# Two node blocks at a time in the node stage of a graph layer

## What is computed

```python
h = maximum(layernorm(x), 0)
edge_in_f = concat([h[src], h[dst], edge_attr]);  msgs_f = relu(edge_in_f @ W1_f + b1_f) @ W2_f + b2_f
agg = segment_sum(msgs_f, dst)
edge_in_r = concat([h[dst], h[src], edge_attr]);  msgs_r = relu(edge_in_r @ W1_r + b1_r) @ W2_r + b2_r
agg = agg + segment_sum(msgs_r, src)
x = x + (h + relu(concat([agg, h]) @ Wn1 + bn1) @ Wn2 + bn2)
```

## Time and profile before

| | us |
|---|---|
| median of three runs | 1609.94 (1607.84 to 1611.34) |
| the profiled execution | 1610.51 |
| its span | 1608.8 |
| PE, PEld busy | 1280.4, 970.6 |
| DVE, ACT, POOL busy | 972.0, 942.1, 1103.2 |

### The profile page before, as it was taken

How to read it: one execution, slowest core, us unless ns; L and a number is a source line. 1 busy time by engine, 2 the same in 40 slices (tenths; PEclk the granted TensorE clock), 3 DMA queues, 4 the chain that set the end, 5 groups by cost and what they waited for, 6 DMA issues and landing times.

```text
span 1608.8 us, 29477 instructions
## 1 busy us (share of the span) xinstructions
PE 1280.4 (80%) x7070; PEld 970.6 (60%) x7070; DVE 972.0 (60%) x3294; ACT 942.1 (59%) x2256; POOL 1103.2 (69%) x1003
## 2 busy tenths in 40 slices
PE   5899998457877778887787877778888756899998
PEld 4677777335655555665565656556666544666665
DVE  7999999426666666666666666666666641222222
ACT  4888888345555555555545555555555524677776
POOL 7888888888888888888888888888888761000000
PEclk9999999768788887778778788887777887999999
DMA  6899998425555555555555555555555547999998
GB/s 214 288 312 315 312 316 290 141 51 111 109 111 111 111 105 104 104 105 105 104 104 105 105 102 100 103 103 103 104 102 101 101 71 235 345 353 343 347 342 298
DMA packets 238410, 281.00 MB, mean 175 GB/s; under 512 B 53170, under 2 KB 155200, under 8 KB 238348
## 3 DMA queue, kind: packets, MB, share of 16 engines
q1 hardware_dynamic: 168408, 241.57, 45.2%
q0 software_dynamic: 68992, 38.59, 20.5%
q10 hardware_dynamic: 948, 0.30, 0.1%
HBM read 162.62 MB, written 117.72 MB: 174 GB/s over the span
## 4 chain that ended last, share of the span: by engine, by line
POOL 33%; issue 22%; DMA 15%; PE 4%; DVE 3%; ACT 1%; POOLq 0%; SPq 0%; DVEq 0%; ACTq 0%
POOL table L532 28%; DMA out_x<-ncentred 12%; POOL got_odd L514 6%; DMA table<-to_send,scatter_at 2%; DVE ncentred L1138 2%; DVE same L979 1%; PE bank L833 1%; PE bank L871 1%; DMA same<-table 1%; PE bank L820 1%; PE bank L882 0%; PE bank L818 0%; SPq L392 0%; PE bank L804 0%; PE bank L892 0%
## 5 line engine op out<-in xcount | busy, mean ns | idle before, releaser
L532 POOL DMA_INDIRECT table<-to_send,scatter_at x392 | 622.6, 1588 | 134.0 <-issue 118.4
L846 PEld LDWEIGHTS bank<-message,same 128*128 128x128 f32 x1960 | 270.3, 222 | 44.2 <-issue 39.2
L846 PE MATMUL bank<-message,same 128*128 128x128 f32 x1960 | 290.9, 313 | 4.8 <-DVE message L1011 4.8
L639 ACT ACTIVATE nh<-nx,all_sums,all_rstd 128x64 f32<-128x64 f32 x784 | 280.2, 434 | 0.1
L514 POOL DMA_INDIRECT got_even<-in_x,gather_first x196 | 212.9, 1086 | 39.8 <-issue 34.7
L775 PE MATMUL bank<-wn_h,nturned 128*128 128x256 f32 x784 | 196.7, 394 | 31.7 <-ACT nhidden L683 24.1
L514 POOL DMA_INDIRECT got_odd<-in_x,gather_at x180 | 180.2, 1001 | 54.9 <-issue 54.0
L804 PE MATMUL bank<-ident,h_ends 128*128 128x128 f32 x196 | 52.0, 359 | 198.7 <-DVE h_ends L1020 192.6
L979 DVE TENSOR_SCALAR_CACHE_REDUCE same<-others,ids 128x128 f32<-128x128 int32 (+3 forms) x392 | 190.7, 543 | 12.7 <-issue 7.9
L818 PE MATMUL bank<-turned,w_ends 128*128 128x256 f32 x392 | 167.1, 516 | 37.9 <-ACT turned_edge L609 37.9
L775 PEld LDWEIGHTS bank<-wn_h,nturned 128*128 128x128 f32 x784 | 143.1, 192 | 67.9 <-issue 36.2
(11 more groups left out here) (79 smaller groups left out, 1984.3 us busy)
## 6 DMA issues: line engine op xcount, KB each, us to landing
nx<-in_x SPq DMA_DIRECT2D x194, 256.0 KB
table<-nhidden SPq DMA_DIRECT2D x97, 512.0 KB
same<-table SPq DMA_DIRECT2D x97, 512.0 KB, 5.4
others<-numbers SPq DMA_DIRECT2D x196, 128.0 KB
out_x<-ncentred SPq DMA_DIRECT2D x97, 256.0 KB, 4.4
nx<-out_x SPq DMA_DIRECT2D x55, 256.0 KB, 4.8
out_x<-nh SPq DMA_DIRECT2D x31, 256.0 KB
table<-to_send,scatter_at POOLq DMA_INDIRECT x392
```

Of the source, the lines that this page charges most:

```text
L532: pool.indirect_dma_start(table, bass.IndirectOffsetOnAxis(ap=scatter_at[s][:, k:k + 1], axis=0), to_send[s][:, k, :], None, compute_op=AL ...
L639: last = act.activation(nh[s][:, g, :], nx[place][:, g, :], ACT.Relu, bias=all_sums[:, at, g:g + 1].rearrange("p a g -> p (a g)"), scale=a ...
L846: last = pe.matmul(bank[6 + s][:, k * M:(k + 1) * M], same[s][:, o, k * P:(k + 1) * P], message[s][:, o, :], start=(o == k), stop=(o == KB ...
```

## The change

Blocks are handled in pairs. Partition p of a pair of blocks holds 16 consecutive nodes: the first 8 belong to block 2i, the others to block 2i + 1. In the node stage SP loads a pair of blocks with one transfer of 512 KB (4 KB for each partition) and stores the table rows of a pair with one of 1 MB (8 KB for each partition). The loads go to four pair buffers `x_pair` in the space of `same`, the rows to four pair buffers `rows_pair` in the space of `kept_more`; `zeros` moves behind them. The first pair is loaded as two single blocks, so that block 0 has its own semaphore. SP loads a pair eight blocks ahead and stores a pair two blocks behind. The last pair has 1696 nodes on LASTP = 106 partitions. The other two stages still move single blocks, now as the halves of a pair. The loops of SP, ACT and DVE in the node stage are unrolled by eight. The diff, cut to its core:

```diff
-    LASTP = (N - (NW - 1) * WIN) // G
+    LASTP = (N - (NW - 2) * WIN) // (2 * G)
+    XRING = 8
...
-        zeros = kept_more[:, 0:2, :].rearrange("p a c -> p (a c)")[:, 0:ZC]
+        rows_pair = [kept_more[:, 4 * p:4 * p + 4, :].rearrange("p a c -> p (a c)") for p in range(XRING // 2)]
+        x_pair = ntab
+        zeros = kept_more[:, 16:18, :].rearrange("p a c -> p (a c)")[:, 0:ZC]
...
-                Step(NW, 0).do(load_x_begin, 0, ring=NRING)
+                for s in range(2):
+                    load_window(x, 0, s, x_pair[0][:, s * G * D:(s + 1) * G * D], b_x_first if s == 0 else b_x[0])
                 load_ends(sp, SRC, src)
...
-                for k in range(1, 6):
-                    Step(NW, 0).do(load_x_begin, k, ring=NRING)
+                for k in range(2, XRING, 2):
+                    Step(NW, 0).do(load_x_begin, k, ring=XRING)
...
-            def last_rows(a):
-                return a[(NW - 1) * WIN:N, :].rearrange("(p g) d -> p (g d)", g=G)
+            def pair_rows(a, i):
+                rows = a[(NW - 2) * WIN:N, :] if is_last(i) else a[bass.ds(i * (2 * WIN), 2 * WIN), :]
+                return rows.rearrange("(p h g) d -> p h (g d)", h=2, g=G)
+
+            def parts(i):
+                return LASTP if is_last(i) else P
 
             def load_window(a, i, s, to, landed):
-                if is_last(i, s):
-                    sp.dma_start(to[0:LASTP, :], last_rows(a)).then_inc(landed, 16)
-                else:
-                    sp.dma_start(to, node_rows(a, i, s)).then_inc(landed, 16)
+                sp.dma_start(to[0:parts(i), :], pair_rows(a, i)[:, s, :]).then_inc(landed, 16)
 
             def store_window(a, i, s, of, stored):
...
+                sp.dma_start(pair_rows(a, i)[:, s, :], of[0:parts(i), :]).then_inc(stored, 16)
...
             def load_x_begin(i, s, turn, place):
                 if not first(turn):
-                    sp.wait_ge(b_centred[s], i - 1)
-                load_window(x, i, s, flat(nx[place]), b_x[place])
+                    for q in range(2):
+                        sp.wait_ge(b_centred[q], i - XRING // 2 + 1)
+                sp.dma_start(x_pair[place // 2][0:parts(i), :], pair_rows(x, i).rearrange("p h c -> p (h c)")
+                             ).then_inc(b_x[place // 2], 16)
...
-            def store_rows(i, s):
-                sp.wait_ge(b_rows[s], 2 * (i + 1))
-                store_window(table[0:N, :], i, s, nhidden[s][:, :], b_stored[s])
+            def store_rows(i, s, turn, place):
+                for q in range(2):
+                    sp.wait_ge(b_rows[q], 2 * (i + 1))
+                sp.dma_start(pair_rows(table[0:N, :], i).rearrange("p h c -> p (h c)"),
+                             rows_pair[place // 2][0:parts(i), :]).then_inc(b_stored[place // 2], 16)
 
             def begin(w):
-                w.do(load_x_begin, 6, ring=NRING)
+                if w.n % 2 == 0:
+                    w.do(load_x_begin, XRING, ring=XRING)
...
-                w.do(store_rows, -1)
+                if w.n % 2 == 0:
+                    w.do(store_rows, -2, ring=XRING)
...
-            run(sp, NW, [(4, 88, 4)], 1, begin)
+            run(sp, NW, [(XRING, 88, XRING)], 1, begin)
...
-                    for q in range(2):
-                        pool.wait_ge(b_stored[q], 16 * (NW // 2))
+                    for q in range(XRING // 2):
+                        pool.wait_ge(b_stored[q], 16 * len(range(q, NW // 2, XRING // 2)))
...
-                    if not first(i):
-                        act.wait_ge(b_stored[s], 16 * i)
-                    act.copy(nhidden[s][:, half * 512:(half + 1) * 512], bank[2 + 2 * s + half][:, :]
-                             ).then_inc(b_rows[s], 1)
+                    if not first(turn):
+                        act.wait_ge(b_stored[place // 2], 16 * turn)
+                    c = (2 * s + half) * 512
+                    act.copy(rows_pair[place // 2][:, c:c + 512], bank[2 + 2 * s + half][:, :]).then_inc(b_rows[s], 1)
```

More of the change, by code:

```diff
@@ L111, in gnn_layer @@
     MORE_FROM = KEPT - MORE
-    assert NW % 2 == 0 and N % G == 0 and G * D == 2 * KB * D and 2 * KEPT <= PAIRS and 4 * KEPT <= NB
+    assert NW % 2 == 0 and N % (2 * G) == 0 and G * D == 2 * KB * D and 2 * KEPT <= PAIRS and 4 * KEPT <= NB
     table = nc.dram_tensor("table", (ROWS, M), F32, kind="Internal").ap()
@@ L255, in gnn_layer @@
         s_loads_held = sem("loads_held")
-        b_x = [sem(f"b_x_in{p}") for p in range(NRING)]
+        b_x = [sem(f"b_x_pair_in{p}") for p in range(XRING // 2)]
+        b_x_first = sem("b_first_x_in")
         b_sums = sems("b_sums_ready")
@@ L269, in gnn_layer @@
         b_rows = sems("b_rows_ready")
-        b_stored = sems("b_rows_stored")
+        b_stored = [sem(f"b_rows_pair_stored{p}") for p in range(XRING // 2)]
         e_means = sem("e_scaled_means_ready")
@@ L371, in load, with is_last @@
                                  ).then_inc(s_others[s], 16)
[L373 to L377, removed]
-            def last_rows(a):
-                return a[(NW - 1) * WIN:N, :].rearrange("(p g) d -> p (g d)", g=G)
+            def is_last(i):
+                return isinstance(i, int) and i == NW // 2 - 1
+            def pair_rows(a, i):
[3 more added lines that the diff above has]
+                return LASTP if is_last(i) else P
             def load_window(a, i, s, to, landed):
-                if is_last(i, s):
-                    sp.dma_start(to[0:LASTP, :], last_rows(a)).then_inc(landed, 16)
-                else:
-                    sp.dma_start(to, node_rows(a, i, s)).then_inc(landed, 16)
+                sp.dma_start(to[0:parts(i), :], pair_rows(a, i)[:, s, :]).then_inc(landed, 16)
             def store_window(a, i, s, of, stored):
[L389 to L392, removed]
+                sp.dma_start(pair_rows(a, i)[:, s, :], of[0:parts(i), :]).then_inc(stored, 16)
             def flat(a):
@@ L692, in begin @@
                     square(0, 0)
-                w.do(copy_rows(0), -1)
-                w.do(copy_rows(1), -1)
+                w.do(copy_rows(0), -1, ring=XRING)
+                w.do(copy_rows(1), -1, ring=XRING)
             for k in range(3):
@@ L702, in _ @@
                     copy_begin(0, 0)
-            run(act, NW, [(4, 92, 4)], 1, begin)
+            run(act, NW, [(XRING, 88, XRING)], 1, begin)
             run(act, NB, [(4, 96, 4)], 2, batch)
@@ L1053, in of_window, with x_window @@
                 return a[:, bass.ds(2 * i + s, 1), :].rearrange("p a g -> p (a g)")
+            def x_window(place):
+                half = place % 2
+                return x_pair[place // 2][:, half * G * D:(half + 1) * G * D].rearrange("p (g d) -> p g d", d=D)
             def sum_begin(i, s, turn, place):
-                dve.wait_ge(b_x[place], 16 * (turn + 1))
-                dve.tensor_reduce(of_window(all_sums, i, s), nx[place][:, :, :], AX.X, ALU.add).then_inc(b_sums[s], 1)
+                if first(turn) and place == 0:
+                    dve.wait_ge(b_x_first, 16)
+                else:
+                    dve.wait_ge(b_x[place // 2], 16 * (turn + 1))
+                dve.tensor_reduce(of_window(all_sums, i, s), x_window(place), AX.X, ALU.add).then_inc(b_sums[s], 1)
             def centre_begin(i, s, turn, place):
@@ L1097, in _ @@
             for k in range(3):
-                Step(NW, 0).do(sum_begin, k, ring=NRING)
-                Step(NW, 0).do(centre_begin, k, ring=NRING)
+                Step(NW, 0).do(sum_begin, k, ring=XRING)
+                Step(NW, 0).do(centre_begin, k, ring=XRING)
                 if k == 0:
@@ L1108, in _ @@
             dve.memset(zeros, 0.0).then_inc(s_zeros, 1)
-            run(dve, NW, [(4, 92, 4)], 0, begin)
+            run(dve, NW, [(XRING, 88, XRING)], 0, begin)
             centre(Step(NB, 0), 0)
```

10 lines of the change are left out of this document (4 added, 6 removed).

## The result

The changed kernel takes 1645.85 us (median; 1644.73 to 1646.32) where the kernel before took 1608.89 on the same chip: a ratio of 1.0227 with a 95% interval of 1.0209 to 1.0244, slower by 37.0 us. Forecast were 1638.0 and slower, with a range to 1648: sign, range and main mechanism hold, and two terms of the sum don't (the layout in the out stage, and the scatter stage). The profiled execution took 1644.73 us, its span 1642.6, 33.8 over the span before. (The medians differ by 3.2 us more than the spans, because the profiled execution of before lies 1.6 us over this median of before, that of the change 1.1 under its own, and 2.1 us lie around its span, where before's had 1.7.)

What follows compares the result with a forecast made beforehand. POOL's 208 gathers, then its scatters, then DMA in the out stage were taken to bound the kernel. 0 + 0.4 + 0 + 27.7 = +28.1 us on 1609.94 gave 1638.0, range 1621 to 1648 (own range 1632 to 1648).

Steps and rivals of the forecast that it cites:

- Part 1: Node stage: larger loads and stores gain 7.3 us of DVE's x waits, hidden before the first scatter: 0, +-3 us.
- Part 2: Start of SP: one more 256 KB load ahead of the gathers' index loads, between 0 and 0.7 us: +0.4.
- part 4: Last pair: 106 partitions use 2 DMA engines; out stage's end +27.7 us (31 at 22.2 GB/s, 39 at 18.7), earlier stages hidden.
- part 3: Later stages: interleaved table rows mean pieces with gaps, packets same in size and number: 0, 3 us to either side.
- The cover: 53 us from the last table store's issue at 287.59 to the first scatter at 340.69, hiding node stage changes.
- POOL's pause: Gathers: one unexplained pause of POOL, 3.49 us at 237.24, which may also come or not.
- an out stage that is slower throughout: Out stage: a sign that the forecast is wrong, pointing to the row layout, for which 0 was taken.
- T96's turn: End of out stage: block 96's table load, issued at 1590.64, gets its turn on the engines at 1595.1.
- the list: End of out stage: step-by-step queue of the last loads and stores on one of two engines, span ending at 1636.5.
- The rival of changing pairs: Last transfers: the two engines change from transfer to transfer, so most overlaps: +11.4, 1621 us; chance 0.08.
- the 106 partitions are spread after all: Rival, six last transfers: 106 partitions get 8 or more engines, all of the 27.7 us goes: 1610.3; chance 0.08.
- the faster rival: 106 partitions spread, and the 7.3 us of x waits on the path as gathers end with the node stage: 1603; chance 0.04.

Runs made afterwards that it cites:

- e6: Kernel before with only the out stage's table loads of blocks 0 to 95 taking 4 KB of every 8 KB: 1620.7 us, 1.0074 times before.
- e7: Kernel before with only the transfers of x + h and out (blocks 0 to 95) using 2 KB of every 4 KB: 1609.3 us, 0.9996 times before.
- e8: Kernel before with table loads of 4 KB out of every 12 KB, neighbouring blocks overlapping: 1606.68 us, 0.999 times before.
- e4: Kernel before without POOL's memset after each gather and without ACT's wait for the last of them: 1822.2 us, 1.1311 times before.
- e2: Kernel before with only the interleaved pair layout (all but the last pair) in all stages, one block at a time: 1620.1 us, 1.0116 times before.
- e3: Kernel before with only its last two blocks as an interleaved pair of 106 partitions each: 1640.49 us, 1.0205 times before.
- e11: Kernel before with only its last two blocks as 106 and 106 partitions, a repeat run: 1638.7 us, 1.0178 times before.
- e12: The changed kernel run again, on the same chip as the repeat with 106 partitions alone: 1647.19 us, 1.0225 times before.
- e1: Changed kernel with each transfer of the last pair cut into 96 and 10 partitions: 1620.02 us, 1.0078 times before.
- e9: Kernel before with POOL's memset after each gather cut from 256 to 128 elements per partition: 1794.3 us, 1.1142 times before.

## Why the prediction was right or wrong

| step | forecast, us | in the profile, us |
|---|---|---|
| to the first scatter (parts 1 and 2) | +0.4 | -3.4 |
| scatter stage (part 4, "hidden") | 0 | +2.6 |
| out stage to T96 (part 3) | 0, 3 to either side | +9.2 |
| from T96 on (part 4) | +27.7 | +25.3 |
| sum | +28.1 | +33.8 |

**Part 1, right in what it is worth, not in how much room there is.** DVE's waits for x fall from 7.3 us to 2.1, which is the first load of all, and the stage ends 10.5 us sooner than in the profile of before; in front of POOL's gathers that is worth nothing. But before's profile is the quickest of its kind. e6, e7 and e8 have its node stage unchanged and issue their last table store at 304.65 to 307.99, where the three kernels with pairs are at 276.9 to 277.2. e6, its last table store (SP in order of time, 255 to 345 us):

```profile
307.99 0.36 SPq L407 DMA_DIRECT2D table<-nhidden  x1
```

and ACT's remote waits there, 30 to 330 us (us in all, times, longest):

```profile
ACT nturned L693 <- remote: 26.1, 12, 4.4
```

These are the waits of e4 in a milder form: 21.2 to 26.1 us in e6, e7 and e8, 24.0 in e2, 9.5 in e3, 31.0 in e11, 1.1 in before's profile and none in the three kernels with pairs. So the pairs may save the node stage some 30 us and not 7.3; whether they prevent these waits, or met three executions without, no run here settles. The cover is 53 us in before's profile and 31 to 34 in e6 to e8. In e11 it is gone: its last two table stores, of 106 partitions, are issued at 316.48 and 319.5, and the first scatter waits for them:

```profile
338.80 1.63 POOL L532 DMA_INDIRECT table<-to_send,scatter_at  x1 [4.29 <-DMA table<-nhidden]
```

In the changed kernel the same transfers are hidden, as forecast, because its node stage ends early.

The -3.4 us of the first scatter are not the node stage's: POOL's pause is there again (4.10 for 3.49), and what became shorter are the gathers. The 196 even ones on the page of before (count, busy us, mean ns):

```profile
L514 POOL DMA_INDIRECT got_even<-in_x,gather_first x196 | 212.9, 1086 | 39.8 <-issue 34.7
```

and of the changed kernel, and of e11, whose node stage is that of before but for its last two blocks:

```profile
L518 POOL DMA_INDIRECT got_even<-in_x,gather_first x196 | 208.8, 1065 | 41.3 <-issue 35.4
```

```profile
L514 POOL DMA_INDIRECT got_even<-in_x,gather_first x196 | 207.1, 1057 | 41.3 <-issue 35.9
```

From one execution to the next the sum moves by as much without the change as with it. Before's profile happened to lie high: the six experiments with single blocks in the node stage (e2, e3, e6, e7, e8, e11) reach the first scatter at 338.55 to 339.47 (e11 after its wait), the three kernels with pairs at 337.34 to 339.08. What is left for larger transfers is 1 us or so, within the 3 us that the range kept.

**Part 2, right.** The first gather starts at 8.50 for 7.81: +0.69, at the end of the bounds (0 to 0.7), with +0.4 taken. Over all profiles the three kernels with pairs start it at 8.39 to 8.71 and the seven with single blocks at 7.63 to 8.10, so the order of SP's loads costs about 0.7 us.

**Part 3, the step that failed.** "Packets stay the same in size and number ... so 0, with 3 us to either side." Size and number did stay, as the counts above show, and the queue still moved 4% less: +9.2 us here, +10.3 in e12, +10.9 in e2, +11.3 in e6. The bound was taken from closed regions, though no row showed another one, so the 3 us were no bound. The prediction named what would show this ("an out stage that is slower throughout") and gave it no chance of its own.

**Part 4, right in its mechanism, its term a little large.** Two completion packets show two engines, and 24.3 GB/s for each is the 24.2 that was taken. Counted from the issue of T96, S92 lands after 21.4 us (forecast 23.9), S94 after 31.2 (34.3), and the end comes after 43.5 (45.9). From S92's landing to the end it is 22.1, forecast 22.0. What was too large is the time until T96's turn: T96 lands 11.8 us after its issue, 9.0 of them its own transfer, so its turn came after 2.8 us, where 4.5 was read from the earlier trace rows. The rest is S91's share of 0.7, which the list put between T96 and T97: they land 9.0 apart. The rival of changing pairs falls: on other engines T97 would have overlapped T96, and S92's 256 KB would not have waited 17.8 us. That the 106 partitions are spread after all falls with the two packets, and the faster rival with the first scatter. The upper end of the range does not follow from its own bounds: at 18.7 GB/s the prediction's 39 us give 1649, without the 3 us beside it, so 1648 was too low an end for them.

By the Trainium skill, page "DMA: Bandwidth & Descriptors", section "Why a DMA increments its semaphore by 16 and not by 1", the number of engines is the largest one up to 16 that divides the outer dimension of both sides of the transfer, and on the queues of SP and ACT the lowest-numbered ones serve. The trace agrees on the number, 2 for 106, and fits the same two serving each time, since T97 lands 9.0 us behind T96. That they are the lowest-numbered no view shows.

**Part 4 in the edge stage, not quite hidden.** POOL's scatters by line, 300 to 1340 us, wait longer for scatters to land. Before:

```profile
L532 POOL DMA_INDIRECT table<-to_send,scatter_at x392 | 622.6, 1588 | 134.0 <-issue 118.4 <-DMA table<-to_send,scatter_at 14.7 <-ACT to_send L625 0.9
```

Changed:

```profile
L536 POOL DMA_INDIRECT table<-to_send,scatter_at x392 | 621.2, 1585 | 138.5 <-issue 118.2 <-DMA table<-to_send,scatter_at 19.0 <-ACT to_send L629 1.2
```

e1:

```profile
L543 POOL DMA_INDIRECT table<-to_send,scatter_at x392 | 620.9, 1584 | 134.2 <-issue 117.9 <-DMA table<-to_send,scatter_at 14.8 <-ACT to_send L636 1.5
```

4.3 us more, of which 2.6 come through, and gone again when the last pair is cut into 96 + 10. The table agrees: with 106 partitions the scatter stage takes 999.71 to 1002.84 us (four profiles), without 995.18 to 997.69 (six). The prediction followed the last store of the edge stage, which is hidden, and left out what the slow transfers do to the scatters beside them. That the scatter's packets wait on the same two engines is argued, not shown.

The three misses (-3.8, +2.6, +9.2) and the tail (-2.4) make up the 5.7 us between the two sums. The time fell into the range because the bounds of other terms were wide enough, not because the layout's cost was foreseen.

## What to carry to other kernels

Ask of every tile shape how many DMA engines it gets, and count them in the trace by the completion packets; a ragged last tile is cheap to cut into parts that divide well (106 into 96 + 10 took 24 us back), and it hurts most where it comes last. One profile shows one execution's slack: the same code had 53 us of cover in one and 31 in another, so take a margin like this from several. An address pattern that no row shows has no bound from rows with another pattern: keep a layout that is read back by a stage at its DMA limit, or run that stage alone first. A stage that ends well before its successor starts can't repay a cost elsewhere, however much better it becomes.

## What the hardware showed that was not expected

- **Distance of pieces.** 4 KB pieces at a distance of 8 KB cost a stage that is bound by DMA 5% of its rate (e6); at 12 KB (e8, where neighbouring loads overlap), or 2 KB pieces at 4 KB (e7), nothing.
- **Issuing can block.** With two engines backed up, SP is held 4.42 and 3.75 us in the issue of a store to all engines, where it takes 0.35. It is so in e3, e11 and e12 too (3.91, 4.04 and 3.90 for S92), and not in e1. The landings came later still, so no row shows that it cost anything.
- **Gathers back to back stop the other engines.** With 0.33 us of memset between the gathers the node stage moves 314 GB/s, 286 to 308 in the six experiments with single blocks, where ACT already has 9.5 to 31.0 us of waits that nothing in the profile ends; with 0.22 us it moves 71 at a DMA share of 0.26 (e9, 60 to 100 us), with none 74 (e4). The DMA engines are idle then, so it is not their rate that runs out; what ACT waits for the profile doesn't name.
